# Graph attention layer on one core: low parts on DVE, counts in 4-bit digits, other load order, cut 125-row transfers

## What is computed

```python
# x: 1250 x 512 (normalised rows), src, dst: 20000 edges, sorted by dst, H = 4 heads of 512 columns
q, k, v = x @ Wq + bq, x @ Wk + bk, x @ Wv + bv          # per head
alpha = (q[dst] * k[src]).sum(-1) / sqrt(512)            # per edge and head
attn = softmax of alpha over the edges of each dst
agg = segment_sum(attn * v[src], dst)
x_attn = agg + x @ Wskip + bskip
h = x_attn @ Wlin + blin + x_attn[:, :512]
h = layernorm(h) * gamma + beta                          # then a second norm and a small gated MLP
```

## Time and profile before

| | us |
|---|---|
| runs (three) | 1184.18, 1184.33, 1184.88; median 1184.33 |
| the profiled execution | 1184.66 |
| its span (first to last instruction) | 1182.5 |
| PE busy | 1094.7 (93%) |
| DVE busy | 599.4 (51%) |
| ACT busy | 329.4 (28%) |
| POOL busy | 171.8 (15%) |
| granted PE clock, mean share of full | 0.974 |

### The profile page before, as it was taken

The page is one execution under the profiler, slowest core; times in us unless marked ns, Lnnn a source line. Parts: engine busy times, 40 slices in busy tenths (PEclk is TensorE's granted clock), DMA queues, the critical chain, the costliest instruction groups (busy, mean ns, idle before and its releaser), DMA issues.

```text
span 1182.5 us, 14807 instructions
## 1 busy us (share of the span) xinstructions
PE 1094.7 (93%) x5666; PEld 896.2 (76%) x5666; DVE 599.4 (51%) x1534; ACT 329.4 (28%) x512; POOL 171.8 (15%) x292
## 2 busy tenths in 40 slices
PE   3789899999999999999999999999999999998861
PEld 2566666677888888888888888888888888877750
DVE  6788788835234333324334332433443234666776
ACT  3353424230233132213222221322232132233210
POOL 4222422220000000000000000000000002534555
PEclk9899899999999999999999999999999999999985
DMA  6534435423001001000100100100010000000101
GB/s 229 166 125 146 139 129 194 165 92 144 1 1 72 1 1 72 1 2 12 61 1 1 72 1 2 32 40 1 1 72 1 1 14 31 18 18 19 35 29 42
DMA packets 13653, 64.41 MB, mean 54 GB/s; under 512 B 1387, under 2 KB 1780, under 8 KB 10001
## 3 DMA queue, kind: packets, MB, share of 16 engines
q1 hardware_dynamic: 8977, 46.67, 11.6%
q0 software_dynamic: 4608, 16.78, 3.8%
HBM read 44.11 MB, written 19.34 MB: 54 GB/s over the span
## 4 chain that ended last, share of the span: by engine, by line
PE 64%; DVE 17%; issue 8%; ACT 5%; DMA 3%; POOL 2%; SPq 0%; POOLq 0%; DVEq 0%; ACTq 0%
PE ps_o L1056 7%; PE ps_o L1057 7%; PE ps_o L1058 7%; PE ps_r L1056 6%; PE ps_r L1057 6%; PE ps_r L1058 6%; PE ps_s L1056 5%; PE ps_s L1058 5%; PE ps_s L1057 5%; DMA acc<-in_x 3%; DVE onehot_src L685 3%; PE ps_t L1261 3%; PE ps_s L1140 2%; DVE opnd_lo L674 1%; DVE prob L1028 1%
## 5 line engine op out<-in xcount | busy, mean ns | idle before, releaser
L1056 PE MATMUL ps_s<-xT_hi,tT 128*128 128x512 f32 (+1 forms) x480 | 175.5, 366 | 0.3 <-DVE top L1013 0.3
L1058 PE MATMUL ps_s<-xT_hi,tT 128*128 128x512 f32 (+1 forms) x480 | 170.1, 354 | 0.0
L1057 PE MATMUL ps_s<-xT_lo,tT 128*128 128x512 f32 (+1 forms) x480 | 169.6, 353 | 0.0
L1056 PE MATMUL ps_o<-y,pT 128*128 128x512 f32 (+1 forms) x400 | 157.8, 394 | 0.0
L1057 PE MATMUL ps_o<-y,pT 128*128 128x512 f32 (+1 forms) x400 | 157.2, 393 | 0.0
L1058 PE MATMUL ps_o<-y,pT 128*128 128x512 f32 (+1 forms) x400 | 157.0, 392 | 0.0
L639 ACT ACTIVATE prob<-prob,nbias 125x1250 f32<-125x1250 f32 x40 | 53.7, 1342 | 255.3 <-DVE nbias L1021 255.3
L1013 DVE CUSTOM_DVE_ANT_0 prob<-ps_s,maskb 125x1250 f32<-125x1250 f32 x40 | 58.2, 1456 | 119.0 <-issue 119.0
L594 ACT ACTIVATE pT<-ps_t 128x500 fp32r<-128x500 f32 (+1 forms) x120 | 58.0, 519 | 203.3 <-PE ps_t L1261 203.3
L879 DVE TENSOR_TENSOR pT<-ps_t,pT 128x500 fp32r<-128x500 f32 (+1 forms) x120 | 67.3, 590 | 93.1 <-ACT pT L594 93.1
L453 POOL MEMSET row_mask<- 18x1 f32 x1 | 0.1, 88 | 709.8 <-DMA xz<-in_mlp_w 709.8
(11 more groups left out here) (244 smaller groups left out, 1977.0 us busy)
## 6 DMA issues: line engine op xcount, KB each, us to landing
products<-prod_parts POOLq DMA_DIRECT2D x32, 512.0 KB, 4.1
gbuf<-products SPq DMA_DIRECT2D x4, 2048.0 KB, 7.8
mbuf<-products SPq DMA_DIRECT2D x4, 2048.0 KB, 7.8
stage<-in_Wq SPq DMA_DIRECT2D x4, 1024.0 KB, 7.9
stage<-in_Wk SPq DMA_DIRECT2D x4, 1024.0 KB, 5.7
stage<-in_Wskip SPq DMA_DIRECT2D x4, 1024.0 KB, 6.2
stage<-in_Wv SPq DMA_DIRECT2D x3, 1024.0 KB, 4.9
stage<-in_Wlin SPq DMA_DIRECT2D x3, 1024.0 KB, 4.7
```

What stands on the lines that cost most here:

```text
L1056: nc.tensor.matmul(out_, a[0], b[0], start=start, stop=False)
L1057: nc.tensor.matmul(out_, a[0], b[1], start=False, stop=False)
L1058: return nc.tensor.matmul(out_, a[1], b[0], start=False, stop=stop)
```

## The change

- `split_lo` leaves POOL. DVE makes the odd low parts too, behind the save of block 0, the even ones still behind block 1.
- `PLANES` is 6, `NP` 209. A PSUM number now holds six counts of 4 bits: the one-hot's value is 16 to the power of the plane, set as an exponent (`weight_i`). The source one-hot is 209 wide. DVE takes even and odd digits apart with two integer operations (`digits`), ACT writes them with two operations and sums the spilled top byte with a third.
- Counts of tile d run beside product d + 1 instead of d. `pack_counts` (the copy) stays at the end of a product, `digits` and `save_counts` stand at block 1 of the product after. Product 0 has no counts, product 10 has.
- SP's first issues are the weights; edge lists and x come behind n = 3. DVE works out the planes (`edge_places`, one small operation less) behind block 1's split of product 0 and the moments (`x_moments`) behind block 2's save.
- Edge lists, x, `xres` and the stores are cut into 112 and 13 rows (`ROW_CUTS`).
- The ring has nine tiles instead of six.
- The scores' third column group uses 125 of the 128 columns of `tT`; the last output tile uses 128 rows instead of 98 (the added rows are zero in `y`).
- `cd_by_rows` waits for the last copy of counts, as `ps_s` is used until then.

```diff
-RING = 6
+RING = 9
+ROW_CUTS = [(0, 112), (112, R - 112)]
-PLANES = 3
+PLANES = 6
 NP = -(-N // PLANES)
...
         @block.sync
-            sp.dma_start(edge_i[0:R, 0, :], src).then_inc(edges_in, 16)
-            sp.dma_start(edge_i[0:R, 1, :], dst).then_inc(edges_in, 16)
             for n in range(2):
                 sp.dma_start(stage[n][:], weights[n][0]).then_inc(stage_in[n], 16)
             sp.dma_start(bcol[:], bias_cols).then_inc(bias_in, 16)
             for n in range(2, 4):
                 sp.dma_start(early[n - 2][:], weights[n][0]).then_inc(early_in[n - 2], 16)
-            sp.dma_start(acc[0:R, :, :], x.rearrange("(t p) n -> p t n", p=R)).then_inc(x_in, 16)
+            for i, ends in enumerate((src, dst)):
+                for a, w in ROW_CUTS:
+                    sp.dma_start(edge_i[a:a + w, i, :], ends[a:a + w, :]).then_inc(edges_in, 16)
+            x_tiles = x.rearrange("(t p) n -> p t n", p=R)
+            for a, w in ROW_CUTS:
+                sp.dma_start(acc[a:a + w, :, :], x_tiles[a:a + w]).then_inc(x_in, 16)
...
+                    for a, w in ROW_CUTS:
+                        sp.dma_start(out[R * done + a:R * done + a + w, :],
+                                     acc[a:a + w, done, :]).then_inc(out_done, 16)
...
         @block.gpsimd
-                    if i == 0 and p + 1 < 3 * H:
-                        split_lo(p + 1)
...
         @block.scalar
+            def pack_counts(d):
+
                 act.wait_ge(onehot_used, sum(len(window(t)) for t in range(d + 1)))
                 if d:
-                    act.wait_ge(count_saved, (PLANES + 1) * d)
+                    act.wait_ge(nibbles_ready, d)
+                    act.wait_ge(count_saved, SUMS * d)
+                nc.scalar.activation(packed[0:R, :], ps_s[0:R, 0:NP], ACT.Copy).then_inc(packed_ready, 1)
+
+            def save_counts(d):
+
+                act.wait_ge(nibbles_ready, d + 1)
+                planes = count[0:R, d, :].rearrange("p (b two n) -> p two b n", two=2, n=NP)
+                for half in range(2):
+                    digits = nibble[half][0:R, :].bitcast(U8).rearrange("p (n b) -> p b n", b=4)
+                    nc.scalar.activation(planes[:, half], digits[:, 0:PLANES // 2, :], ACT.Copy,
+                                         accum_out=planesum[0:R, d, half:half + 1]).then_inc(count_saved, 1)
...
+                    if i == 1 and 1 < p <= NT + 1:
+                        save_counts(p - 2)
...
-                if p < NT:
-                    save_counts(p)
+                if 0 < p <= NT:
+                    pack_counts(p - 1)
...
         @block.vector
+            def digits(d):
+
+                dve.wait_ge(packed_ready, d + 1)
+                if d:
+                    dve.wait_ge(count_saved, SUMS * d)
+                nc.vector.tensor_scalar(nibble[0][0:R, :], packed[0:R, :], NIBBLES, None, ALU.bitwise_and)
+                nc.vector.tensor_scalar(nibble[1][0:R, :], packed[0:R, :], 4, NIBBLES, ALU.logical_shift_right,
+                                        ALU.bitwise_and).then_inc(nibbles_ready, 1)
...
                 for i in range(KC):
-                    if p < NT:
-                        onehots(p, part(p, i))
+                    if i == 1 and 1 < p <= NT + 1:
+                        digits(p - 2)
+                    if 0 < p <= NT:
+                        onehots(p - 1, part(p - 1, i))
                     save_product(p, [i])
-                    if i == 1 and p + 1 < 3 * H:
-                        split_lo(p + 1)
+                    if i < 2 and p + 1 < 3 * H:
+                        split_lo(p + 1, 1 - i)
+                    if p == 0 and i == 1:
+                        edge_places()
+                    if p == 0 and i == 2:
+                        x_moments()
...
         @block.tensor
-                    if p < NT:
-                        count_part(p, i)
+                    if 0 < p <= NT:
+                        count_part(p - 1, i)
...
-                        ins = mm3(ps_s[:, c:c + w], [tT[g % 2][:, s, k, d % GT, :] for s in range(2)],
+                        m = P if w == BANK else R
+                        ins = mm3(ps_s[0:m, c:c + w], [tT[g % 2][:, s, k, d % GT, 0:m] for s in range(2)],
                                   [xT[s][:, k, c:c + w] for s in range(2)], k == 0, k == KC - 1)
...
-                    rows = P if t < NS - 1 else LAST_ROWS
-                    ins = mm3(ps_o[:, :], [pT[d % 2][0:rows, s, t, :] for s in range(2)],
-                              [y[0:rows, s, t, :] for s in range(2)], t == 0, t == NS - 1)
+                    ins = mm3(ps_o[:, :], [pT[d % 2][:, s, t, :] for s in range(2)],
+                              [y[:, s, t, :] for s in range(2)], t == 0, t == NS - 1)
```

More of the change, by code:

```diff
@@ L149, in graph_layer @@
         edge_p = put("edge_p", [P, 2, ET], F32)
-        plane = [put(f"plane{i}", [P, ET], F32) for i in range(2)]
-        packed = put("packed", [P, NP + 1], I32)
+        at_plane = put("at_plane", [P, ET], F32)
+        packed = put("packed", [P, NP], I32)
+        nibble = [put(f"nibble{i}", [P, NP], I32) for i in range(2)]
+        spill = put("spill", [P, NP], BF16)
         bcol = put("bcol", [P, 4, H * KC], F32)
@@ L513, in split_hi @@
                         nc.scalar.activation(opnd[n % 4][0][:], raw(n)[:], ACT.Copy).then_inc(hi_ready[odd], 1)
-            def save_counts(d):
+            def pack_counts(d):
                 act.wait_ge(onehot_used, sum(len(window(t)) for t in range(d + 1)))
                 if d:
-                    act.wait_ge(count_saved, (PLANES + 1) * d)
[L521 to L527, removed]
+                    act.wait_ge(nibbles_ready, d)
[8 more added lines that the diff above has]
+                                         accum_out=planesum[0:R, d, half:half + 1]).then_inc(count_saved, 1)
+                top_byte = packed[0:R, :].bitcast(U8).rearrange("p (n b) -> p b n", b=4)[:, 3, :]
+                nc.scalar.activation(spill[0:R, :], top_byte, ACT.Copy,
+                                     accum_out=planesum[0:R, d, 2:3]).then_inc(count_saved, 1)
             act.wait_ge(consts_ready, 1)
@@ L713, in save_product @@
                     ins.then_inc(prod_free, 1)
-            dve.wait_ge(edges_in, 32)
-            link(nc.vector.tensor_copy(edge_f[0:R], edge_i[0:R]))
-            source = edge_f[0:R, 0, :]
-            for i in range(2):
-                link(nc.vector.tensor_scalar(plane[i][0:R, :], source, float(NP * (i + 1)), None, ALU.is_ge))
-            link(nc.vector.scalar_tensor_tensor(out=edge_p[0:R, 0, :], in0=plane[0][0:R, :], scalar=-float(NP),
-                                                in1=source, op0=ALU.mult, op1=ALU.add))
@@ L728, in _, with edge_places @@
-            dve.wait_ge(ids_ready, 1)
-            split_lo(0)
+            def edge_places():
+                dve.wait_ge(edges_in, 32 * len(ROW_CUTS))
+                dve.wait_ge(ids_ready, 1)
+                link(nc.vector.tensor_copy(edge_f[0:R], edge_i[0:R]))
+                source, place = edge_f[0:R, 0, :], at_plane[0:R, :]
+                link(nc.vector.tensor_scalar(place, source, -float(NP // 2), 1.0 / NP, ALU.add, ALU.mult))
+                link(nc.vector.tensor_scalar(place, place, ROUND, None, ALU.add))
+                link(nc.vector.tensor_scalar(place, place, ROUND, None, ALU.subtract))
+                nc.vector.scalar_tensor_tensor(out=edge_p[0:R, 0, :], in0=place, scalar=-float(NP), in1=source,
+                                               op0=ALU.mult, op1=ALU.add)
+                link(nc.vector.tensor_scalar(weight_i[0:R, :], place, 4 * 2.0 ** 23, ONE_BITS, ALU.mult, ALU.add))
@@ new lines, in x_moments @@
+            def x_moments():
+                dve.wait_ge(x_in, 16 * len(ROW_CUTS))
+                for t in range(NT):
+                    nc.vector.bn_stats(stats[0:R, t, :], acc[0:R, t, :]).then_inc(dve_step, 1)
+                    steps[0] += 1
+                dve.wait_ge(dve_step, steps[0])
+                for t in range(NT):
+                    ins = nc.vector.bn_aggr(mv[0:R, t, :], stats[0:R, t, :])
+                ins.then_inc(ln_var, 1)
+            split_lo(0, 0)
+            split_lo(0, 1)
@@ L779, in _ @@
                             skip_lo(i)
-                if p == 0:
-                    dve.wait_ge(x_in, 16)
-                    for t in range(NT):
-                        nc.vector.bn_stats(stats[0:R, t, :], acc[0:R, t, :]).then_inc(dve_step, 1)
-                        steps[0] += 1
-                    dve.wait_ge(dve_step, steps[0])
-                    for t in range(NT):
-                        ins = nc.vector.bn_aggr(mv[0:R, t, :], stats[0:R, t, :])
-                    ins.then_inc(ln_var, 1)
                 if p == 1:
```

51 lines of the change are left out of this document (22 added, 29 removed).

## The result

The kernel after takes 1168.85 us (median of four, 1162.59 to 1169.78), the kernel before 1184.26 beside it (1183.39 to 1184.88). The ratio is 0.9857, 95% interval 0.9843 to 0.9871. The forecast was 1156.5: the direction was right and the time lies in the range, but only some 55% of the gain came. The profiled executions took 1169.78 and 1184.66 us.

What follows compares the result with a forecast made beforehand. PE was taken to bound the heads, x's transfer the start, and POOL-stretched one-hots to stall the products. Terms -12.3 - 13.1 + 0.5 - 1.2 - 0.7 - 1.1 = -27.9 gave 1156.5 us, range 1140 to 1170.

Steps and rivals of the forecast that it cites:

- Start: Up to product 2: earlier weights and x's faster cut transfer bring product 2 to 64.2 instead of 76.5 us, -12.3.
- rival (c): At the start: the cut doesn't make x come sooner, moments begin at 42.1; 1167.5 us, chance 0.08.
- Products 2 to 10: Product stage: no one-hots stretched by POOL, cheaper tiles and counts, stalls behind DVE's splits; 158.3 against 171.4 us, -13.1.
- rival (b): In the one-hots: their cost is fixed, so tiles stay at 0.46 us despite fewer columns; 1170 us, chance 0.08.
- the forecast's 158.3: Products 2 to 10: PE's own work of 138.1 us plus stalls of 15.7 and 4.5 us.
- To the first head: Behind product 10: it gets counts, which DVE's copy of 1.2 us at its head delays; +0.5 us.
- Heads: Score matmuls with 125-column weights give -1.2 us, output matmuls of 128 instead of 98 rows -0.7.
- PE is the bound there, so both count whole: In the heads: savings of 1.2 and 0.7 us in matmuls shorten the whole time in full.
- Tail and end: Last store cut in two: less than the 3.6 us wait for the transfer after the last add, -1.1 us.
- xres halves are fetched beside DVE's work: In the tail: the cut fetch of xres overlaps DVE's work; no term in the sum.
- (a): In the products: nine tile buffers let DVE run ahead and PE's queue absorbs the stalls; -20, 1136 us, chance 0.10.
- (d): Products 2 to 10: POOL doesn't stretch the one-hots, so moved splits only load DVE; slower, 1190 us, chance 0.05.

Runs made afterwards that it cites:

- uncut kernel: The kernel after with x and the edge lists fetched in one transfer of 125 rows each; 1176.76 us.
- the kernel with the exact place and full weights: The kernel after with large buffers at exactly the addresses of before and all score matmuls on 128-column weights; 1162.4 us.

## Why the prediction was right, and where it was off

**Start** (-12.3, measured -11.8). First matmul 12.7 against 13.8, moments at 30.45 against 31.1, product 2 at 64.7 against 64.2: right step by step. The uncut kernel shows that the cut carries it, so rival (c) is out. Product 0's end and DVE's queue of edge places, save and moments came as worked out.

**Products 2 to 10** (-13.1, measured -11.0). The mechanism was right: POOL's split was what stretched the one-hots (seven of them in the trace of before, not eight: of the ten splits two met bias operations, and the one at 241.75 us met none), and stalls of about 2 us behind DVE's splits took their place. Two sizes were off. A tile takes 0.41 us, not 0.36: 208 columns fewer save 0.05 us, so the slope drawn from src at 417 and dst at 125 columns gave twice too much; rival (b) was half true. A count matmul was 0.09 us instead of 0.112, which gave some back: with the clock near 1.00 throughout this stretch took 157.5 us (the kernel with the exact place and full weights), 0.8 from the forecast's 158.3. What is missing is the clock. I had left it out because no POOL split would open a gap of over 3 us. In after it fell to 0.50, the lower level, behind two of the stalls that I forecast myself, for which PE's waits are 1.06 us (ended at 112.08) and 0.59 us (ended at 152.30):

```profile
113.60:116.50 2.90, 2.90 (x8) 2.26 (x8) 2.69 (x12) 0.00 (x0) 0.69 (x1) 0.50 0.94 356
154.30:157.60 3.30, 3.30 (x9) 2.62 (x8) 2.19 (x11) 0.00 (x0) 0.69 (x1) 0.50 1.06 405
```

6.2 us at half the clock cost some 3 us, the difference between 160.5 and 157.5. But such a stall isn't enough by itself: the kernel with the exact place and full weights has the same two (1.07 us, ended at 111.43, and 0.48 us, ended at 150.26) and keeps 1.00 behind them:

```profile
112.00:118.00 6.00, 5.69 (x28) 4.41 (x28) 4.77 (x21) 1.48 (x5) 0.84 (x2) 1.00 0.62 243
151.00:157.00 6.00, 5.72 (x28) 4.51 (x29) 4.75 (x21) 0.84 (x2) 0.99 (x2) 1.00 0.96 334
```

What decides between the two stays open.

**To the first head** (+0.5, measured +2.9). Most of it goes with the clock: the same program took 80.4 us at 1.00 (the uncut kernel) where after took 83.6, with 20 busy us at 0.83 that had 0.91 in before. The place of the buffers is worth some 0.6 us of it: at 1.00 and the old place this stretch took 79.8 (the kernel with the exact place and full weights).

**Heads** (-1.9 in all, measured +1.1 for each, +4.5 in all). The two terms of the sum came out near what was forecast (1.1 and 0.7 us for 1.2 and 0.7, measured with the buffers in place). What failed is the step "PE is the bound there, so both count whole": nothing else was thought to move. The edit of a buffer that no head's matmul uses moved their operands behind it (tT, pT, y, mbuf; not xT) by 32 bytes, which costs 1.55 us a head, 6.2 in all. I read the length of count in the diff and counted no cost for it. The 6 ns that I had taken as a penalty of 125-wide weights at 512 columns is the same size as what a place costs; which of the two it is wasn't tested.

**Tail and end** (-1.1 and the heads' share, measured +2.0). The last transfer is awaited 1.5 us instead of 3.6, so the end gave 2.1, twice the forecast. But "xres halves are fetched beside DVE's work" counted only the transfer and not what it releases. POOL's wait gives 4.5 us in the median, and that is my price for the meeting of the two operations.

**Rivals.** (a) stays out: nine buffers gain nothing over six. (b) is half true in its size. (c) and (d) are refuted by one kernel each. None of them held the causes that took the gain. That 1168.85 still lies in the range is luck in part: the room up to 1170 was left for (b) and (c). The parts as measured are 14.1 for POOL's splits and 7.9 for x's cut, 1.8 for narrow weights and full rows, 2.1 at the end; against them 6.6 for the place (6.2 of it seen in the heads) and 4.5 for the tail. That makes 14.8 of the 15.4 us, though parts measured one at a time need not add up, and each median carries some us by the clock of its executions.

## What to carry to other kernels

Keep large buffers at their addresses when a small one in front grows, or compare the interval of equal matmuls between the two traces: a few ns each, 0.8 us a head in the 240 score matmuls of 512 columns and 0.7 us in the 120 that stream mbuf, were worth 6.2 us in the heads here. A faster transfer off the path isn't free: ask what it releases, and beside what that will run; fix the order with a wait on the event that matters. When a stall stands behind a long operation in one engine's order, move what the bound engine waits for in front of it before making either faster.

## What was not expected of the hardware

- A 512-column f32 matmul with 128-column weights starts every 0.227 or every 0.234 us at the same granted clock, by its operands' addresses alone. Moves of the buffers behind `xT` by 32, 64 and 128 bytes all cost something, from 0.9 to 1.6 us a head, most of it in the score matmuls and those that stream mbuf (0.226 at the old place, 0.235 at +32). Which operand and which rule it is wasn't separated.
- DVE's COPY of 4 elements and TENSOR_TENSOR of 12 take 0.17 us alone and 0.91 and 1.18 beside POOL's addition of 1.28 us, while the 1250-column operation on ps_s keeps its 1.46. The Trainium skill ("SBUF — State Buffer", "SBUF: two separate sides") describes an exclusive lock on a port pair, held for a whole instruction; the rows of 0.91 and 1.18 us end with POOL's instruction, within 0.03 us, and agree.
- The granted clock was 0.83, 0.91 or 1.00 in the same 20 us of busy work behind product 10 in different executions. Of the four executions of after, the one of 1162.59 us had a mean granted clock of 0.978 over its span, the others (1168.17 to 1169.78) 0.971 or 0.972. Differences of a few us between medians here should be read in the stages, not in the totals.
